# Turning the feed-forward tokens tile by tile in a one-core Perceiver block, with the first four products in halves of 256 tokens

## What is computed

```python
h = _ln(x, g1, beta1)
...                                                        # causal linear attention, 16 heads of 64
attn = jnp.moveaxis(outs, 0, 1).reshape(b, s, H * DH) @ wo
x = x + attn
h2 = _ln(x, g2, beta2)
x = x + (jax.nn.gelu(h2 @ w1 + b1, approximate=False) @ w2 + b2)   # w1: 512 x 2048, w2: 2048 x 512
```

## Time and profile before

| | |
|---|---|
| Time, median of 3 runs | 699.74 us (698.71 to 931.4) |
| The profiled execution's own time | 702.32 us |
| Its span in the profile | 700.6 us |
| Mean granted TensorE clock over the span | 0.968 of full speed |
| Busy share of the span | PE 93%, PEld 77%, DVE 61%, ACT 53%, POOL 36% |
| Chain of work that ended last | PE 78%, DVE 12%, ACT 3%, issue 3%, DMA 2% |

### The profile page before, as it was taken

How to read it: one execution, slowest core, us unless ns; L and a number is a source line. 1 busy time by engine, 2 the same in 40 slices (tenths; PEclk the granted TensorE clock), 3 DMA queues, 4 the chain that set the end, 5 groups by cost and what they waited for, 6 DMA issues and landing times.

```text
span 700.6 us, 9558 instructions
## 1 busy us (share of the span) xinstructions
PE 651.6 (93%) x3370; PEld 538.0 (77%) x3371; DVE 426.5 (61%) x688; ACT 372.8 (53%) x523; POOL 252.9 (36%) x172
## 2 busy tenths in 40 slices
PE   4979998998998999989969999969999999999994
PEld 4868886886876788878758888768888888888883
DVE  8566666656677545576776354845475463762775
ACT  4499986986973254430142244322574555754850
POOL 5078885776894424340000022123022020220233
PEclk9999998998999999999989999969999999999998
DMA  8435453343041612221080793316599191991925
GB/s 324 187 120 175 148 182 129 121 138 118 9 143 60 198 61 90 83 98 62 1 279 22 242 403 120 120 46 238 182 353 373 53 360 46 356 371 66 341 84 176
DMA packets 51844, 116.95 MB, mean 167 GB/s; under 512 B 5208, under 2 KB 5208, under 8 KB 48736
## 3 DMA queue, kind: packets, MB, share of 16 engines
q1 hardware_dynamic: 47360, 106.51, 43.2%
q10 hardware_dynamic: 3168, 5.77, 2.4%
q0 software_dynamic: 1280, 4.20, 1.8%
HBM read 102.31 MB, written 14.16 MB: 166 GB/s over the span
## 4 chain that ended last, share of the span: by engine, by line
PE 78%; DVE 12%; ACT 3%; issue 3%; DMA 2%; POOL 1%; SPq 0%; POOLq 0%; DVEq 0%; ACTq 0%
PE bank L1351 18%; PE bank L1353 18%; PE bank L1352 18%; PE bank L1365 5%; PE bank L1416 3%; PE bank L1417 3%; PE bank L1384 3%; PE bank L1385 3%; PE bank L1750 1%; PE bank L1580 1%; PE bank L1401 1%; PE bank L1730 1%; PE bank L1568 1%; DVE xn L984 1%; PE bank L1737 1%
## 5 line engine op out<-in xcount | busy, mean ns | idle before, releaser
L466 POOL TENSOR_TENSOR nat_lo<-raw,nat_hi 128x512 fp32r<-128x512 f32 x104 | 134.3, 1315 | 55.9 <-ACT nat_hi L584 55.3
L515 POOL TENSOR_TENSOR e_lo<-e_raw,e_hi 128x2048 fp32r<-128x2048 f32 x9 | 41.6, 4619 | 230.2 <-ACT e_hi L743 230.2
L863 DVE TENSOR_TENSOR ct_lo<-bank,ct_hi 128x512 fp32r<-128x512 f32 x96 | 65.9, 689 | 48.7 <-ACT ct_hi L551 48.4
L1351 PE MATMUL bank<-w_hi,turned 128*128 128x512 f32 x176 | 70.7, 402 | 4.0 <-DVE turned L990 2.6
L551 ACT ACTIVATE ct_hi<-bank 128x512 fp32r<-128x512 f32 x96 | 57.1, 596 | 26.4 <-PE bank L1365 24.5
L1352 PE MATMUL bank<-w_lo,turned 128*128 128x512 f32 x176 | 69.5, 395 | 0.0
L1353 PE MATMUL bank<-w_hi,turned 128*128 128x512 f32 x176 | 69.4, 394 | 0.0
L584 ACT ACTIVATE nat_hi<-raw 128x512 fp32r<-128x512 f32 x104 | 65.0, 629 | 0.0
L1365 PE MATMUL bank<-ident,raw 128*128 128x128 f32 x384 | 61.1, 285 | 0.0
L1351 PE MATMUL bank<-e_hi,turned 128*128 128x512 f32 x144 | 59.0, 409 | 1.5 <-issue 1.5
L1365 PEld LDWEIGHTS bank<-ident,raw 128*128 128x128 f32 x384 | 50.1, 147 | 12.7 <-issue 1.2
(11 more groups left out here) (252 smaller groups left out, 1449.8 us busy)
## 6 DMA issues: line engine op xcount, KB each, us to landing
raw<-in_ctx_dram SPq DMA_DIRECT2D x24, 1024.0 KB, 5.0
w_raw<-in_L_ffn_w_dram SPq DMA_DIRECT2D x24, 1024.0 KB, 5.4
e_raw<-in_L_ffn_wo_dram SPq DMA_DIRECT2D x16, 1024.0 KB, 7.4
w_raw<-in_L_attn_w_dram SPq DMA_DIRECT2D x8, 1024.0 KB, 5.2
e_raw<-in_L_ffn_w_dram SPq DMA_DIRECT2D x8, 1024.0 KB, 7.4
slots_x<-zeros SPq DMA_DIRECT2D x1, 4096.0 KB, 16.9
slots_y<-zeros SPq DMA_DIRECT2D x1, 3840.0 KB, 26.2
vectors<-slots_x ACTq DMA_DIRECT2D x11, 256.0 KB, 5.0
```

Of the source, the lines that this page charges most:

```text
L466: nc.gpsimd.tensor_tensor(nat_lo[:, j, :], raw[b % 2][:, j, :], nat_hi[:, j, :].bitcast(f32), ALU.subtract).then_inc(nat_lo_ready, 1)
L515: nc.gpsimd.tensor_tensor(e_lo[j][:, :, :], e_raw[j][:, :, :], e_hi[j][:, :, :].bitcast(f32), ALU.subtract).then_inc(e_lo_ready[j], 1)
L863: nc.vector.tensor_tensor(ct_lo[:, n % CR, :], src, ct_hi[:, n % CR, :].bitcast(f32), ALU.subtract).then_inc(t_lo, 1)
L1351: nc.tensor.matmul(dst, lh, rh, start=first and k == 0, stop=False)
```

## The change

- PE: `tile_turned` takes a second set of banks (6, 7, 5, 4). Normalised tiles 0 and 1 are turned between `heads_transposed(3)` and `projected(3, 0)`. The feed-forward's first four products are each done in two halves of 256 tokens (`up_half`). The first halves need only tiles 0 and 1. Tile 2 is turned behind the first two of them, tile 3 behind the fourth, then come the four second halves. Products write banks 0 to 3 in turn, and `up_whole(n)` waits for gelu n - 4. After the four: down 0, 1, 2, then up 4, down 3, up 5, down 4 and so on.
- DVE: `gained` of tiles 0 and 1 moves in between the last tile's `divided`. `lower_turned` of tiles 0 and 1 goes behind `tile_stats` of tile 2, that of tile 2 between `tile_stats` and `gained` of tile 3, and that of tile 3 behind it.
- ACT: `upper_turned` for tiles 0 and 1, then `split_w(9)`, tile 2, `split_w(10)`, tile 3.

```diff
+        TURN_BANK2 = [bank[6], bank[7], bank[5], bank[4]]
...
+            upper_turned(0, 1)
+            upper_turned(1, 1)
             split_w(9)
-            upper_xT(1)
+            upper_turned(2, 1)
             split_w(10)
+            upper_turned(3, 1)
...
-                nc.scalar.activation(gl[n % 2][:, :], bank[n % 2][:, :], ACT.Gelu, bias=b1_col[:, n:n + 1]).then_inc(gelu_ready, 1)
+                nc.scalar.activation(gl[n % 2][:, :], bank[n % 4][:, :], ACT.Gelu, bias=b1_col[:, n:n + 1]).then_inc(gelu_ready, 1)
...
                 masked(4 * t + 2)
                 masked(4 * t + 3)
+                if t == NT - 1:
+                    dve.wait_ge(vec_loaded, 80)
+                    dve.wait_ge(oT_done, 2 * (NT - 1))
+                    gained(x1n, 0, NT + 3)
                 divided(4 * t + 2)
+                if t == NT - 1:
+                    gained(x1n, 1, NT + 4)
                 divided(4 * t + 3)
             attended(NT - 2)
             lower_oT(NT - 1)
             dve.wait_ge(xa_ready, NT - 1)
             tile_stats(x1n, NT - 2)
-
-            dve.wait_ge(vec_loaded, 80)
+            lower_turned(0, 1)
+            lower_turned(1, 1)
             dve.wait_ge(oT_done, 2 * NT)
-            for t in range(NT - 1):
-                gained(x1n, t, NT + 3 + t)
+            gained(x1n, NT - 2, 2 * NT + 1)
             attended(NT - 1)
             dve.wait_ge(xa_ready, NT)
             tile_stats(x1n, NT - 1)
-
+            lower_turned(2, 1)
             gained(x1n, NT - 1, 2 * NT + 2)
-            lower_xT(1)
+            lower_turned(3, 1)
             split_w(9)
             split_w(10)
...
             heads_transposed(NT - 1)
+            tile_turned(0, 1)
+            tile_turned(1, 1)
             for part in range(4):
                 projected(NT - 1, part)
 
-            pe.wait_ge(xa_ready, NT)
-            transpose_xn(1)
+            def up_half(n, half):
+
+                u, some = 8 + 2 * (n // 4), slice(2 * P * half, 2 * P * (half + 1))
+                if n == 0:
+                    pe.wait_ge(xT_lo_ready, 2 * NT if half else NT + 2)
+                    pe.wait_ge(*lower(u))
+                if n == NT - 1:
+                    pe.wait_ge(xa_ready, NT)
+                return product(bank[n % 4][:, some], columns(u, n % 4), [(hi[:, some], lo[:, some]) for hi, lo in xT])
+
+            for n in range(4):
+                up_half(n, 0)
+                if n == 1:
+                    tile_turned(2, 1)
+            tile_turned(3, 1)
+            for n in range(4):
+                up_half(n, 1).then_inc(up_done, 1)
...
-                if n >= 2:
-                    pe.wait_ge(gelu_ready, n - 1)
-                product(bank[n % 2][:, :], columns(u, n % 4), xT).then_inc(up_done, 1)
+                pe.wait_ge(gelu_ready, n - 3)
+                product(bank[n % 4][:, :], columns(u, n % 4), xT).then_inc(up_done, 1)
...
-            for n in range(WHOLE + 1):
+            for n in range(3):
+                down(n)
+            for n in range(4, WHOLE + 1):
                 up_whole(n)
-                if n >= 1:
-                    down(n - 1)
+                down(n - 1)
```

More of the change, by code:

```diff
@@ L665, in _, with upper_turned @@
                     upper_values((s - 6) // NKT, (s - 6) % NKT)
-            def upper_turned(t):
-                act.wait_ge(xT_done, t + 1)
-                nc.scalar.activation(xT_hi[:, :, t * P:(t + 1) * P], TURN_BANK[t][:, :].rearrange("p (k n) -> p k n", n=P),
+            def upper_turned(t, norm=0):
+                act.wait_ge(xT_done, NT * norm + t + 1)
+                nc.scalar.activation(xT_hi[:, :, t * P:(t + 1) * P], (TURN_BANK, TURN_BANK2)[norm][t][:, :].rearrange("p (k n) -> p k n", n=P),
                                      ACT.Copy).then_inc(xT_hi_ready, 1)
[L673 to L676, removed]
             def value_heads(n):
@@ L985, in first_gained, with lower_turned @@
                 nc.vector.scalar_tensor_tensor(xn[:, t, :], xn[:, t, :], roots[:, t, 1:2], shift, ALU.mult, ALU.add).then_inc(xn_ready, 1)
-            def lower_turned(t):
-                dve.wait_ge(xT_hi_ready, t + 1)
-                nc.vector.tensor_tensor(xT_lo[:, :, t * P:(t + 1) * P], TURN_BANK[t][:, :].rearrange("p (k n) -> p k n", n=P),
+            def lower_turned(t, norm=0):
+                dve.wait_ge(xT_hi_ready, NT * norm + t + 1)
+                nc.vector.tensor_tensor(xT_lo[:, :, t * P:(t + 1) * P], (TURN_BANK, TURN_BANK2)[norm][t][:, :].rearrange("p (k n) -> p k n", n=P),
                                         xT_hi[:, :, t * P:(t + 1) * P].bitcast(f32), ALU.subtract).then_inc(xT_lo_ready, 1)
@@ L1056, in _ @@
                 normalise(x1n, xt, t, roots[:, t, 0:1])
[L1057 to L1060, removed]
             dve.wait_ge(proj_hi_ready, 1)
@@ L1489, in _, with tile_turned @@
             xT = [(xT_hi[:, k, :], xT_lo[:, k, :]) for k in range(KD)]
-            def tile_turned(t):
-                pe.wait_ge(xn_ready, t + 1)
-                if t == NT - 1:
+            def tile_turned(t, norm=0):
+                pe.wait_ge(xn_ready, NT * norm + t + 1)
+                if t == NT - 1 and norm == 0:
                     pe.wait_ge(xT_lo_ready, 1)
                 for k in range(KD):
-                    mm = nc.tensor.transpose(TURN_BANK[t][:, k * P:(k + 1) * P], xn[:, t, k * P:(k + 1) * P], ident[:, :])
+                    mm = nc.tensor.transpose((TURN_BANK, TURN_BANK2)[norm][t][:, k * P:(k + 1) * P], xn[:, t, k * P:(k + 1) * P], ident[:, :])
                 mm.then_inc(xT_done, 1)
@@ L1533, in _ @@
                 value_product(n)
[L1535 to L1542, removed]
             def columns(u, m):
```

## The result

The changed kernel takes 689.83 us (median of 4 runs, 685.66 to 691.38) against 699.23 us for the kernel before in the same rounds (697.96 to 699.74, and one outlier of 931.4). The ratio is 0.986, with a 95% interval of 0.982 to 0.991. That is between 6.4 and 12.9 us less; the prediction had 8.1 less, 691.6.

The account below looks back on a forecast made before the run. PE's own work bounds the kernel (78% of the chain). Gap -7.85, half clock -2.9, `gl_lo` wait -0.6, narrower matmuls +0.6, transposes +0.9, new stall +1.6: 8.1 us off 699.74 gives 691.6, range 689.6 to 698.5.

Parts of the forecast that it names:

- Tiles 0 and 1 in the gap: Ahead of the last projection: eight transposes fit PE's 0.98 us wait for `oT_lo`; late heads cost 0 to 0.1 us.
- First halves with no wait: Behind the last projection: first half products start at 351.40 without a wait, 0.120 us per 256-column matmul.
- The chain of tile 3: Ahead of the second halves: `gained(3)` queues behind tile 2's difference on DVE; PE stands 1.6 us for tile 3.
- Down 0 with no wait: First down product: starts at 365.5, PE and DVE's `gl_lo` being ready within 0.1 us of each other.
- Half clock -2.9: First up products: 24 matmuls no longer run at half clock, 5.44 us instead of 8.3, so 2.9 us less.
- Four banks: Feed-forward products: four banks instead of two take away a PE wait that cost nothing.
- The whole gain reaches the end: Behind the changed stretch: later weights, router and experts follow PE's progress, so all 8.1 us shorten the total.
- The clock did not fall again: Rival: behind the new 1.6 us stall the clock falls again, costing 1.6 to 2.9 us, 693.3 to 694.5; chance 0.17.
- The weight load hides: Rival, half products: the load no longer hides, 0.217 us per matmul, 9.3 us more, 700.9, gain gone; chance 0.06.
- Narrow matmuls at a quarter of the rate: Rival, half products: 256 columns cost 0.427 us per matmul, 29.5 us more, 721.1 us, slower by 3%; chance 0.08.
- the lost gain: Rival, behind the stretch: weights come by the DMA queue's clock and take the gain back, about 698.5 us; chance 0.05.

Follow-up runs that it names:

- the filled waits: The kernel before, with 24 extra matmuls whose results nobody reads placed in PE's waits ahead of the feed-forward: 696.39 us against 698.94, ratio 0.996.
- the quarters: The changed kernel with the first four products in pieces of 128 columns instead of halves of 256: 712.4 us, one execution.
- the change again: The changed kernel with no edit, measured in more rounds: 690.72 us against 698.94 for the kernel before, ratio 0.988.

## Why the prediction was right or wrong

**The step that failed.** It is the last one, behind the sum: "2% (14 us) is about what a measurement of this kernel can tell from no change, so this counts as the same", with 0.89 for it. No row stood behind the 2%; of the three times known then, the two that were no outliers lay 1.03 us apart (698.71 and 699.74). The runs showed otherwise: with 2 to 12 executions of a kernel the interval here is about 0.25 to 0.5% to each side, and three measurements of the change gave 0.982 to 0.991, 0.986 to 0.991 and 0.984 to 0.991, each wholly below 1. So a gain of 1.2% is seen plainly, and my own sum forecast just that. The mechanism held, with one cause in it half wrong (tile 3, below).

**The sum.** 8.1 us forecast; 7.9 to 8.0 by the stretch in three traces; 9.4, 8.2 and 7.1 by the medians. Its terms, one by one:

- *Tiles 0 and 1 in the gap: 0 to 0.1.* Right, 0. The last `divided` ends 0.29 us before the heads are turned (336.11 + 0.42 against 336.82), where it was 0.40 before. I had let the second `gained` push it by 0.43, and it was pushed by 0.11: I had added listed lengths, but the next instruction starts up to 0.1 us ahead of the listed end of the one before (the `gained` pair costs 1.45 us from start to start, not 1.50, and a `divided` 0.74, not 0.84). What I did not say is what the place hides besides the transposes: late, it costs 2.4 to 2.7 us.
- *First halves with no wait, 0.120 per matmul.* Right: 12 matmuls from 344.42 to 345.86, 0.120.
- *The chain of tile 3.* The stall was 1.41, forecast 1.6, in the place and with the releaser that I named. From the last first half to the first second half it was 2.2 us, as forecast (2.15); the 0.2 us lie in where the transposes are taken to end. The reason was half wrong. I wrote as if `gained(3)` behind tile 2's lower part made the stall, with PE ready at about the same time (357.6 against 357.7; measured, 350.61 against 350.70). Moving `gained(3)` forward took 0.2 us and left the stall; moving PE's transposes and ACT's copy too took nearly all of it. The stall is there because tile 3 is turned behind all first halves, with nothing left for PE to do while ACT and DVE finish it.
- *Down 0 with no wait, DVE just in time.* PE did not wait. DVE's `gl_lo` was done at about 358.2, 0.4 us ahead: a little more slack than my 0.1. From the weight differences on DVE took 5.55 us (352.68 to 358.23) where I had 5.7, and PE's second halves took 5.85 where I had 5.75.
- *Half clock -2.9.* The mechanism is shown by the filled waits (2.4 to 2.6). The size is that of one execution: two others with the same wait of 2.88 us lost 2.7 and 1.7, so that it fitted the medians is in part luck. The clock was 1.00 in all three traces of the changed kernel behind a stall of 1.41 us.
- *Four banks: nothing.* As a wait for banks, nothing; the order of products that they allow is worth the 0.4 us of `gl_lo`, which stands in the sum.
- *The whole gain reaches the end.* Right, by the table, within its 1.5 us.

**The rivals.** The clock did not fall again (0.17), in this kernel; in the quarters it fell behind a stall of the same length. The weight load hides at 256 columns: a matmul costs 0.112 us at 128 columns and 0.120 at 256, not the sum of both. That rules out 0.217, and with it that a load overlaps only where the row groups differ, as the Trainium skill ("TensorE: Matmul & The Clock Gate", Part 3, what overlaps and what doesn't) has it. Its formula for a load (section "LDWEIGHTS") gives 107 ns for 128 columns, near the 112 measured between two matmuls of 128 columns. Narrow matmuls at a quarter of the rate did not happen: 256 columns took 0.120, not 0.427. That 66 columns fit four cycles was chance: 128 columns cost the same 0.11. And the row of plain fp32 that I read as four cycles of 2.4 GHz per column stands in a stretch at half clock, which I had not looked up:

```profile
465.00:470.00 5.00, 5.00 (x24) 5.00 (x25) 4.07 (x22) 0.00 (x0) 2.31 (x2) 0.50 0.14 52
```

So its 0.211 us are two cycles of 1.2 GHz per column, not four of 2.4 GHz, and about what a matmul of 128 columns cost at half clock in the quarters (0.214). In the trace of the change again, 7 of these matmuls touch the microsecond from 457 (clock 0.50), and 12 that from 459 (clock 1.00). Nothing in the rows spoke for a quarter of the rate but the 66 columns.

**The range.** 689.6 to 698.5 held the time, near its lower end; it was wide upwards for the clock and the lost gain, neither of which came.

## What to carry to other kernels

Doing the steps of a chain tile by tile gains little as long as the consumer still waits for the last tile: here its first product started only 0.5 us earlier, and the 2.4 of 8 us that this kernel won came mostly from the clock and the order of products. The larger part comes from cutting the consumer's first products, so that it works on the early tiles meanwhile. Before calling a gain too small to measure, take the scatter from runs of the kernel itself. When an operation is put into such a stretch, leave work of the consumer behind it: the transposes of the last tile cost a wait of 1.41 us where nothing stood behind them, and no more than 0.15 us where one half product (1.44 us) did. Cut no narrower than where a matmul's columns still cover its cost per matmul (0.11 us here, reached between 128 and 256 columns), and price the slow clock behind a stall along with the stall.

## What was not expected of the hardware

The span of one and the same kernel scatters with the clock's falls in places that the change does not touch: the stretch from 115 to 125 us had a clock of 1.00 in one trace of the changed kernel, and its last heads stand at 336.82, 342.10 and 342.58 in three. One profiled pair would have given 16.7 us for a gain of 8. The same wait of 2.88 us ahead of the feed-forward was followed by 2.9, 2.7 and 1.7 us lost to half clock. And with pieces of 128 columns, once the clock was at half, it stayed there for 23 us with PE busy, while in the kernel before it was back some 7 us after it fell in this place (358.4 to 365.2). Why is open, as only one execution shows it.
